# Low parts of K and of the turned context by minus the identity on TensorE, copied out by ScalarE, with V one slot later

## The reference

```python
q = (layernorm(x) @ Wq);  k = context @ Wk;  v = context @ Wv      # 16 heads of 16
attn = softmax(q @ k.T * 0.25)                                     # 112 x 375 for each of 16 x 16
x = x + tanh(g_xattn[0]) * ((attn @ v) @ Wo)
x = x + tanh(g_ffn[0]) * moe(layernorm(x))                         # 8 experts, top 2
```

## Time and profile before

| what | us |
|---|---|
| median of 3 runs | 598.87 (597.97 to 600.97) |
| the profiled execution, its own time | 595.91 |
| its span, first to last instruction | 594.2 |
| attention steps with everything in them (4 to 15) | about 17.9 each |

### The profile page before, as it was taken

The page is one execution under the profiler, slowest core; times in us unless marked ns, Lnnn a source line. Parts: engine busy times, 40 slices in busy tenths (PEclk is TensorE's granted clock), DMA queues, the critical chain, the costliest instruction groups (busy, mean ns, idle before and its releaser), DMA issues. The chain is left out here.

```text
span 594.2 us, 15127 instructions
## 1 busy us (share of the span) xinstructions
PE 486.9 (82%) x4723; PEld 436.3 (73%) x4724; DVE 427.8 (72%) x902; ACT 339.8 (57%) x638; POOL 293.2 (49%) x252
## 2 busy tenths in 40 slices
PE   4873989999999999999989721697899999999920
PEld 3762878888888888888868621487789999999920
DVE  5962789999989989989997669577776555555510
ACT  4731556667676657767654681667665555545410
POOL 9403654545654555654545422706547565555440
PEclk9996899999999999999995955699999999999985
DMA  8676446665466465546332076855624443343233
GB/s 205 180 192 147 107 114 168 168 171 122 99 179 162 93 175 151 131 108 147 75 71 79 25 275 195 298 199 155 168 37 73 74 62 53 62 71 53 28 39 130
DMA packets 69022, 74.88 MB, mean 126 GB/s; under 512 B 28744, under 2 KB 57248, under 8 KB 68784
## 3 DMA queue, kind: packets, MB, share of 16 engines
q1 hardware_dynamic: 60912, 63.23, 39.8%
q0 software_dynamic: 8064, 11.06, 11.3%
HBM read 42.51 MB, written 14.98 MB: 97 GB/s over the span
## 5 line engine op out<-in xcount | busy, mean ns | idle before, releaser
L358 POOL TENSOR_TENSOR PL<-PT 125x448 f16<-125x448 f32 x96 | 100.8, 1052 | 133.0 <-ACT PT L489 133.0
L489 ACT ACTIVATE PT<-bank 125x448 f32<-125x448 f32 x192 | 104.0, 544 | 89.1 <-PE bank L623 88.3
L781 DVE TENSOR_REDUCE mx<-bank 112x1 f32<-112x375 f32 x256 | 130.8, 542 | 29.5 <-PE bank L608 28.1
L1235 POOL DMA_INDIRECT acc_scr<-ys,slot_row x42 | 69.1, 1645 | 83.4 <-ACT ys L1292 74.6
L608 PE MATMUL bank<-KS,QS 97*112 97x376 f32 x256 | 90.9, 376 | 13.3 <-DVE mx L781 10.7
L623 PE MATMUL bank<-QS,KS 98*125 98x256 f32 x384 | 84.2, 304 | 6.2 <-DMA QS<-nm 5.1
L623 PEld LDWEIGHTS bank<-QS,KS 98*125 98x125 f32 x384 | 67.1, 194 | 7.5 <-DMA QS<-nm 5.6
L1354 PE MATMUL bank<-xH,GH 128*128 128x256 f16 x336 | 65.7, 278 | 7.6 <-ACT sg L1277 5.9
L1354 PE MATMUL bank<-xL,GH 128*128 128x256 f16 x336 | 65.3, 277 | 0.0
L1354 PE MATMUL bank<-xH,GL 128*128 128x256 f16 x336 | 65.2, 276 | 0.0
L608 PEld LDWEIGHTS bank<-KS,QS 97*112 97x112 f32 x256 | 45.5, 182 | 26.1 <-DVE mx L781 22.2
(11 more groups left out here) (215 smaller groups left out, 1078.0 us busy)
## 6 DMA issues: line engine op xcount, KB each, us to landing
KS<-kH SPq DMA_DIRECT2D x128, 94.0 KB, 2.2
KS<-kL SPq DMA_DIRECT2D x64, 94.0 KB, 2.2
QS<-q_scr SPq DMA_DIRECT2D x96, 56.0 KB
ctx_sb<-in_ctx SPq DMA_DIRECT2D x16, 281.2 KB
wsq<-in_L_ffn_gate_w SPq DMA_DIRECT2D x8, 512.0 KB, 3.7
wsq<-in_L_ffn_up_w SPq DMA_DIRECT2D x8, 512.0 KB, 4.6
w_raw<-in_L_ffn_gate_w SPq DMA_DIRECT2D x8, 512.0 KB, 6.2
w_raw<-in_L_ffn_up_w SPq DMA_DIRECT2D x8, 512.0 KB, 4.2
```

Of the source, the lines that this page charges most:

```text
L358: pool.tensor_tensor(PL[:, 2 * k:2 * k + 2, :, 0:N], PT[:, 2 * k:2 * k + 2, :, 0:N], PH[:, 2 * k:2 * k + 2, :, 0:N], ALU.subtract).then_in ...
L489: act.activation(PT[:, 2 * k:2 * k + 2, :, 0:N].rearrange("p a e i -> p (a e) i"), psST[k % 2][0:JP].rearrange("p (a i) -> p a i", i=NI)[: ...
L781: dve.tensor_reduce(mx[:, hd:hd + 1], psS[hd % 2][0:N, 0:M], AX.X, ALU.max).then_inc(v_max, 1)
L1235: pool.indirect_dma_start(acc_scr, bass.IndirectOffsetOnAxis(ap=slot[:, TH * t + k:TH * t + k + 1].bitcast(U32), axis=0), ys[:, u, k, :], ...
```

## The change

PE makes the low parts now. After ACT has copied `kH` out of `misc`, PE adds minus the identity times `kH` onto K, which still stands in `misc`, so what is left there is the low part; ACT copies it out to `kL`. The same is done for the turned context. Slots of the new pieces: `k_rest` on PE 3 (behind both scores of the slot), `key_low` on ACT 3 (behind the exponential), `ctx_rest` on PE 12 (ahead of `project_o`), `transposed_low` on ACT 13. `project_v` goes to slots 5, 6, 7, so the copy to `vf` goes from slot 7 to 8. `V1` and `VR` go from 3 to 4, while `V2`, `LV` and `SQ` stay. The first batch's parts, and the turned context of the second, are still made on DVE. `Wf["o"]` lies over a part of `kL`, which makes room for `minus`.

```diff
+        minus = sb("minus", [128, 128], F32R)
-        Wf = {k: first(f"w{k}_f", [p, 2, DIM], F32) for k, (_, p) in shapes.items()}
+        Wf = {k: first(f"w{k}_f", [p, 2, DIM], F32) for k, (_, p) in shapes.items() if k != "o"}
+        Wf["o"] = f32(kL[:, NB - 1, :, 0:DIM])
...
-        VP = (4, 5, 6)
+        VP = (5, 6, 7)
+        KR, KL, TR, TL = 3, 3, 12, 13
...
-        V1, VR, V2, LV = 3, 3, 6, 6
+        V1, VR, V2, LV = 4, 4, 6, 6
...
+        of_k = lambda b: 2 * b - 1
+        of_ctx = lambda b: 2 * b - 2
...
+                def key_low(i, c):
+                    b, h, u = at(i, c)
+                    act.wait_ge(p_R, of_k(b))
+                    act.activation(kL[:, u], misc[:].rearrange("p (m n) -> p m n", m=2)[:, :, 0:MP],
+                                   ACT.Copy).then_inc(a_R, 1)
+
+                def transposed_low(i, c):
+                    b, h, u = at(i, c)
+                    act.wait_ge(p_R, of_ctx(b))
+                    act.activation(cTL[:, :, 0:M], misc[0:CK].rearrange("p (c n) -> p c n", c=2)[:, :, 0:M],
+                                   ACT.Copy).then_inc(a_R, 1)
...
+                        if k == KL and live(i, c, 0):
+                            key_low(i, c)
+                        if k == TL and live(i, c, -1):
+                            transposed_low(i, c + 1)
                         if k == V1 and live(i, c, 1):
...
+                act.wait_ge(s_id, 1)
+                act.activation(minus[:], ident[:], ACT.Copy, scale=-1.0)
                 w_high("q")
...
-                    if m == 0:
+                    if m == 0 and isinstance(b, int) and b < 2:
                         pe.wait_ge(v_T, b + 1)
+                    elif m == 0:
+                        pe.wait_ge(a_R, of_ctx(b))
...
+                def k_rest(i, c):
+
+                    b, h, u = at(i, c)
+                    pe.wait_ge(a_K, b + 1)
+                    for m in range(2):
+                        mm = pe.matmul(misc[:, 512 * m:512 * m + MP], minus[:], kH[:, u, m, :],
+                                       start=False, stop=True, skip_group_check=True)
+                    mm.then_inc(p_R, 1)
+
+                def ctx_rest(i, c):
+
+                    b, h, u = at(i, c)
+                    pe.wait_ge(a_T, b + 1)
+                    for k in range(2):
+                        mm = pe.matmul(misc[0:CK, 512 * k:512 * k + MP], minus[0:CK, 0:CK], cTH[:, k, :],
+                                       start=False, stop=True, skip_group_check=True)
+                    mm.then_inc(p_R, 1)
...
+                    if t == 0 and starts(i, c):
+                        pe.wait_ge(v_K, 1)
+                    elif t == 0:
+                        pe.wait_ge(a_R, of_k(b))
...
+                        if s == KR and live(i, c, 0):
+                            k_rest(i, c)
+                        if s == TR and live(i, c, -1):
+                            ctx_rest(i, c + 1)
                         if s == MT and live(i, c, 1):
...
-                        if s == KP[-1] + 1 and live(i, c, 0):
-                            key_low(i, c)
...
-                        if s == CT + 1 and live(i, c, -1) and not starts(i, c):
-                            transposed(i, c + 1)
```

More of the change, by code:

```diff
@@ L270, in keys @@
                     for s, t in enumerate((kH, kH, kL)):
-                        sp.wait_ge(v_K if s == 2 else a_K, b + 1)
+                        if s < 2:
+                            sp.wait_ge(a_K, b + 1)
+                        elif starts(i, c):
+                            sp.wait_ge(v_K, 1)
+                        else:
+                            sp.wait_ge(a_R, of_k(b))
                         for g in range(4):
@@ L573, in ctx_T @@
                         for t in range(JT):
[L574 to L575 removed]
+                            mm = pe.matmul(misc[0:CK, 512 * k + JP * t:512 * k + JP * (t + 1)],
+                                           ctx_sb[:, u, t, CK * k:CK * (k + 1)], ident[0:JP, 0:JP],
+                                           start=(t == 0), stop=(t == JT - 1), is_transpose=True)
                     mm.then_inc(p_T, 1)
```

8 lines of the change are left out of this document (3 added, 5 removed).

## The result

| | before | after |
|---|---|---|
| median of the runs beside each other | 598.42 us (4 runs) | 616.18 us (614.88 to 617.25, 4 runs) |
| span of the profiled execution | 594.2 us | 614.0 us |
| mean granted clock in it | 0.921 | 0.917 |

The changed kernel takes 1.0305 times as long, interval 1.0262 to 1.0348: 18 us more. The forecast was 609.5 (600.0 to 614.5). The direction was right; the loss is 17.8 where 10.6 was forecast, outside the range. In every table a ratio goes by the undisturbed runs of a kernel alone and a median by all of them, which is why the two can stand apart, in cast_early by 1.4 per cent.

A forecast was written before the change was run, and what follows sets the result against it. PE and DVE were taken to wait on each other in turn, neither the sole bound. Square steps +11.2 and steps without a square -0.6 gave +10.6 us on 598.9, so 609.5, range 600.0 to 614.5.

The forecast's parts named there:

- What leaves DVE is worth at most PE's 0.9 a step: Two subtractions leave DVE, about 1.7 us a step; they can give PE at most its 0.9 of waits.
- PE gets 0.68, `cTH` makes it wait up to 0.35: Two new matmul pairs on PE, 0.34 us each; the second may wait up to 0.35 for `cTH`.
- Square steps, +1.4 each by one chain through ACT, POOL and PE: Eight steps: `kL` copy delays square, casts, exponential 6 and POOL's low part 8; +11.2 us in all (4 to 15).
- Steps without a square, -0.1 each, -0.6 in all: Steps 2, 3, 7, 10, 13, 15: DVE's freed time slightly outweighs PE's new work.
- the low end: Steps without a square: -0.2 us each if all PE's waits for DVE vanish; the other end is +1.0.
- the late chain: Steps without a square: ACT's new copy and later V chain about a microsecond late, still in time for slot 8.
- Step 1 costs nothing: Step 1 has no exponentials, so its chain has no hold on PE: 0 within 0.3 us.
- Worse than forecast: Rival: `cTH` wait in every step, PE's 0.68 lost without squares too; +19 us, 618; chance 0.09.
- DVE's relief: Rival at the maxima in slots 0 to 8: waits between PE and DVE vanish; -7 us, 592; chance 0.10.
- the chain's bounds: Eight square steps at +0.5 to +1.9 us each, 4 to 15 in all, less 0.6 for the other steps.

The follow-up runs named there:

- cast_early: The changed kernel with V1 and VR back at slot 3, so ACT casts `VS<-vf` ahead of the square; 615.1 us, 1.0125 times the kernel before.
- ctx_only: The kernel before with only the turned context's low part made on PE and copied out by ACT; 598.4 us, 1.0034 times the kernel before.
- square_out: The changed kernel with the square cut from 2048 columns to 8; 605.1 us, 1.0096 times the kernel before.
- before_cast_late: The kernel before with V1 and VR at slot 4, the cast `VS<-vf` behind the square; 604.8 us, 1.0093 times the kernel before.
- k_only: The kernel before with only K's low part made on PE and copied by ACT, V in slots 5 to 7; 613.6 us, 1.0269 times the kernel before.

## Why the prediction was wrong

- *What leaves DVE is worth at most PE's 0.9 a step*: right as a bound, but little of it was there to be had. The 0.9 is an average. In steps 7, 10 and 13 of before PE waited 0.23 and 0.32 us for maxima, and in after 0.23 and 0.35. What went is a third wait of about 0.54 in the square steps, and there PE stood for exponentials instead. With the square in slot 4 no square step of a kernel with the change was shorter than before's. Where the Trainium skill's page "Perfetto Trace Analysis", section "Optimizing Scalar/DVE Operations", says that moving work from a saturated DVE to Scalar may help, ctx_only speaks against it here, where part of the work went to PE: DVE was busy 171.6 us of 200 in place of 181.5, and the steps from 4 on took 0.15 to 0.26 more.
- *PE gets 0.68, `cTH` makes it wait up to 0.35*: `ctx_rest` (192.38) did not wait in the step shown, nor in any of steps 2 to 14 of after. In ctx_only it waited 0.17 to 0.18 in steps 5 to 13 and 0.32 in 2 and 3, and the 0.15 to 0.26 a step that this kernel loses is below one pair's 0.34.
- *Square steps, +1.4 each by one chain through ACT, POOL and PE*: right in mechanism and, link by link, within 0.1 us down to POOL's subtraction. square_out takes the loss away with the square, before_cast_late gives half of it with the cast alone. The size was +1.56. Beyond the +1.4 lies one term, POOL's `VS<-vr`, which took 2.38 and not 1.69 with DVE's low part (188.78, 0.61) beside it; 0.40 of these 0.69 came back, as the low part 8 behind it took 0.99 and not 1.39. Eight steps: 12.5 where 11.2 was forecast.
- *Steps without a square, -0.1 each, -0.6 in all*: **this step failed.** Those up to 13 gave +4.7: step 2 +2.9, steps 3, 7, 10 and 13 +1.8. I stayed near the low end, at which PE's waits for DVE vanish; in 7, 10 and 13 they did not (0.55 before, 0.58 after). And I named the late chain here ("late here by about a microsecond too, but still in time for slot 8") and looked only at slot 8. It was POOL's low part 8 that came late, in every one of these steps: PE waited for it 2.70 us in step 2, with the clock falling behind the wait, 0.89 in step 3 and 0.73 in 7, 10 and 13. Moving the cast `VS<-vr` takes this wait away, and with it 2.4 us of step 2 and 0.2 of each of 7, 10 and 13. k_only loses as much in 7, 10 and 13 without a wait for POOL, with a longer one for a maximum, so what makes up the rest was not isolated. The end of the loop's body has no part in it, since before pays for it as well.
- *Step 1 costs nothing*, and no term for what follows step 15: +0.85 and +1.3 (step 15 itself, credited with -0.1, lies in the second). At the start `kH` of step 1 came 1.5 us later (41.14, 39.66) and step 1 was 0.6 shorter. What makes these up was not tried.
- *The rivals.* "Worse than forecast" had 618 by `cTH` and PE's 0.68 in every step; the time was near, the mechanism was not this. DVE's relief did not win, in any run.
- *The range* took the chain's bounds for its own and left nothing for a long wait with a fall of the clock behind it. In the spans the loss is 19.8, 9.2 more than forecast: 5.3 from the steps without a square (4.7 and the 0.6 credited), 1.2 from those with one, 2.2 from the two ends, 0.5 from the rest of the program. The medians differ by 2.0 less than the spans.

What stays open: the rest of the loss in steps 7, 10 and 13 and that in step 3; step 1 and the steps behind 15; why the clock fell behind some waits of about 1 us and not behind others of the same length; why before's slot 4 for the square cost it half a microsecond in undisturbed steps; and whether an order exists that uses the change's relief and beats before. None of the 18 kernels did.

## What to carry to other kernels

A relief on one engine is worth what its partner waits for it, and its price is where the work goes in the other engine's list: count every instruction that now stands ahead of the next one that somebody waits for, and on POOL and DVE what will run beside it. When an instruction is moved, look up who waits for it in every list: SyncE's wait for `wsq` turned a gain of 1.5 us a step into single losses of 5. Before a difference is put down to a cost such as a loop's end, look whether the kernel before pays it too. And sum the steps by kind, the first and last ones too: here over a third of the loss lay outside the eight steps that I had worked out.
